# Scaling the exponentials of attention on ScalarE in place of VectorE, in the last group of heads

## The reference

```python
q, k, v = (einsum('bsd,hed->bhse', x, W) for W in (W_Q, W_K, W_V))
scores = einsum('bhse,bhme->bhsm', q, k) / sqrt(128)
scores = where(causal, -1e9, scores)
pattern = softmax(scores, axis=-1)
z = einsum('bhsm,bhme->bhse', pattern, v)
x = layernorm(x + einsum('bhse,hde->bsd', z, W_O))
```

## Time and profile before

| | before |
|---|---|
| median of 3 runs | 1580.17 us (1578.04 to 1580.86) |
| the profiled execution | 1575.68 us, span 1573.5 us |
| TensorE matmul busy | 1489.1 us (95%) |
| VectorE busy | 1122.9 us (71%) |
| ScalarE busy | 744.3 us (47%) |
| GpSimd busy | 504.1 us (32%) |
| chain that ended last | TensorE 47%, issue 22%, VectorE 13%, GpSimd 12%, ScalarE 5% |

### The profile page before, as it was taken

The page is one execution under the profiler, slowest core; times in us unless marked ns, Lnnn a source line. Parts: engine busy times, 40 slices in busy tenths (PEclk is TensorE's granted clock), DMA queues, the critical chain, the costliest instruction groups (busy, mean ns, idle before and its releaser), DMA issues.

```text
span 1573.5 us, 29159 instructions
## 1 busy us (share of the span) xinstructions
PE 1489.1 (95%) x9433; PEld 1303.9 (83%) x9433; DVE 1122.9 (71%) x3031; ACT 744.3 (47%) x1967; POOL 504.1 (32%) x355
## 2 busy tenths in 40 slices
PE   6999999999999988999999999999899799999997
PEld 5989888888989877887888888878688688988886
DVE  5878787887878777655657777867977736442697
ACT  5666666666656544343532263325232544454221
POOL 3323222222322101432347324633673413000650
PEclk9999999999999999999999999999999899999999
DMA  7564646463656203666676457646574788798884
GB/s 274 201 218 169 247 168 228 153 230 136 243 174 222 87 1 130 196 188 178 213 223 203 158 175 218 214 144 193 174 213 167 221 279 286 243 301 265 288 262 143
DMA packets 129737, 315.87 MB, mean 201 GB/s; under 512 B 15968, under 2 KB 39216, under 8 KB 128608
## 3 DMA queue, kind: packets, MB, share of 16 engines
q1 hardware_dynamic: 125024, 301.95, 58.5%
q0 software_dynamic: 4608, 12.59, 2.4%
HBM read 225.35 MB, written 88.60 MB: 200 GB/s over the span
## 4 chain that ended last, share of the span: by engine, by line
PE 47%; issue 22%; DVE 13%; POOL 12%; ACT 5%; DMA 1%; SPq 1%; DVEq 0%; ACTq 0%; POOLq 0%
PE psum L511 40%; POOL act_sb L836 6%; POOL mix L854 3%; POOL xs L866 2%; PE psum L1741 2%; DVE s_sb L1322 1%; PE psum L1752 1%; ACT p_sb L968 1%; PE psum L1731 1%; PE psum L1980 1%; ACT kT_hi L927 1%; DVE s_sb L1320 1%; POOL square_sum L858 1%; DVE kT_lo L1201 1%; DVE pT_lo L1337 1%
## 5 line engine op out<-in xcount | busy, mean ns | idle before, releaser
L511 PE MATMUL psum<-xT_hi,gu_w 128*128 128x512 f32 x1088 | 373.1, 402 | 12.4 <-DVE act_sb L1372 11.6
L836 POOL TENSOR_TENSOR act_sb<-act_sb,comb 128x512 f32<-128x512 f32 x96 | 158.1, 1646 | 375.3 <-DVE act_sb L1372 300.2
L511 PEld LDWEIGHTS psum<-xT_hi,gu_w 128*128 128x128 f32 x1088 | 205.4, 189 | 65.3 <-DVE act_sb L1372 13.2
L1009 ACT ACTIVATE gated<-psum 128x512 f32<-128x512 f32 (+1 forms) x138 | 82.4, 597 | 369.3 <-PE psum L511 367.0
L1372 DVE TENSOR_TENSOR act_sb<-psum,gated 128x512 f32<-128x512 f32 (+1 forms) x138 | 94.9, 688 | 169.9 <-PE psum L511 162.3
L790 POOL TENSOR_TENSOR split_stage<-raw_stage,split_stage 128x768 fp32r<-128x768 f32 x56 | 103.0, 1839 | 351.2 <-ACT split_stage L917 351.2
L511 PE MATMUL psum<-xT_lo,gu_w 128*128 128x512 f32 x544 | 215.5, 396 | 0.0
L511 PEld LDWEIGHTS psum<-d_w,act_hi 128*128 128x128 f32 (+1 forms) x1104 | 149.8, 188 | 13.2 <-issue 1.5
L511 PE MATMUL psum<-d_w,act_hi 128*128 128x256 f32 (+1 forms) x1104 | 154.2, 282 | 0.0
L966 ACT ACTIVATE p_sb<-s_sb,neg_max 128x128 f32<-128x128 f32 x128 | 51.5, 403 | 171.5 <-DVE neg_max L1322 171.3
L511 PEld LDWEIGHTS psum<-xT_lo,gu_w 128*128 128x128 f32 x544 | 102.7, 189 | 18.7
(11 more groups left out here) (257 smaller groups left out, 4021.6 us busy)
## 6 DMA issues: line engine op xcount, KB each, us to landing
gu_w<-w_split SPq DMA_DIRECT2D x138, 512.0 KB, 3.9
w_split<-split_stage SPq DMA_DIRECT2D x56, 768.0 KB, 4.0
d_w<-w_split SPq DMA_DIRECT2D x138, 256.0 KB, 4.0
bw<-l_w SPq DMA_DIRECT2D x63, 496.0 KB, 3.7
xs<-zeros SPq DMA_DIRECT2D x21, 1280.0 KB, 7.5
raw_stage<-w_all SPq DMA_DIRECT2D x56, 384.0 KB, 4.5
decay_all<-decay_dram SPq DMA_DIRECT2D x32, 384.0 KB, 5.5
in_w<-w_split SPq DMA_DIRECT2D x40, 256.0 KB, 4.2
```

The source lines that it names most:

```text
L511: last = nc.tensor.matmul(out_ap, w, m, start=start and n == 0, stop=stop and n == len(pairs) - 1, **kw)
L836: pool.tensor_tensor(act_sb[:, s % 2, :], act_sb[:, s % 2, :], comb[:, comb_block(s) % 2, :], ALU.mult).then_inc(comb_done, 1)
L1009: act.activation(gated[to, s % 2, :], psum[0:to.stop - to.start, G_BANK, :], ACT.Silu).then_inc(gated_ready, 1)
```

## The change

In the last group alone (norm is True there), VectorE keeps the reciprocal but no longer scales. ScalarE scales instead, with two ACTIVATE instructions of the function Identity whose scale is the column row_inv. They stand behind the exponentials of unit i and scale unit i-1; before them ScalarE waits for the reciprocal of unit i-1 (r_ready). The second signals p_scaled, as VectorE's second did.

```diff
--- before.py
+++ after.py
@@ -967,6 +967,11 @@
                                        accum_out=row_sum[:, u % 3, 0:1])
                         act.activation(p_sb[:, u % 3, P:3 * P], s_sb[:, u % 2, P:3 * P], ACT.Exp, bias=neg_max[:, u % 3, 1:2], scale=-1.0,
                                        accum_out=row_sum[:, u % 3, 1:2]).then_inc(p_ready, 1)
+                    if norm and 0 <= i - 1 < UNITS:
+                        u = i - 1
+                        act.wait_ge(r_ready, g * UNITS + u + 1)
+                        act.activation(p_sb[:, u % 3, 0:P], p_sb[:, u % 3, 0:P], ACT.Identity, scale=row_inv[:, u % 3, 0:1])
+                        act.activation(p_sb[:, u % 3, P:3 * P], p_sb[:, u % 3, P:3 * P], ACT.Identity, scale=row_inv[:, u % 3, 1:2]).then_inc(p_scaled, 1)
                     for bp, j in jobs:
                         qkv_high(g, bp, j)
                     if u_t is not None:
@@ -1326,9 +1331,10 @@
                         dve.wait_ge(p_ready, g * UNITS + u + 1)
                         dve.reciprocal(row_inv[:, u % 3, :], row_sum[:, u % 3, :]).then_inc(r_ready, 1)
                         dve.wait_ge(r_ready, g * UNITS + u + 1)
-                        dve.tensor_scalar(p_sb[:, u % 3, 0:P], p_sb[:, u % 3, 0:P], row_inv[:, u % 3, 0:1], None, ALU.mult)
-                        dve.tensor_scalar(p_sb[:, u % 3, P:3 * P], p_sb[:, u % 3, P:3 * P], row_inv[:, u % 3, 1:2], None,
-                                          ALU.mult).then_inc(p_scaled, 1)
+                        if not norm:
+                            dve.tensor_scalar(p_sb[:, u % 3, 0:P], p_sb[:, u % 3, 0:P], row_inv[:, u % 3, 0:1], None, ALU.mult)
+                            dve.tensor_scalar(p_sb[:, u % 3, P:3 * P], p_sb[:, u % 3, P:3 * P], row_inv[:, u % 3, 1:2], None,
+                                              ALU.mult).then_inc(p_scaled, 1)
                     for bp, j in jobs:
                         qkv_low(g, bp, j)
                     if u_t is not None:
```

## The result

The change takes 1590.24 us (median of 4 runs, 1589.08 to 1591.45), the kernel before 1579.41 (4 runs, 1578.04 to 1580.86): a ratio of 1.0073, 95% interval 1.0060 to 1.0086, or 10.8 us slower. The forecast was 1590.3 with +10.1 us.

What follows compares the result with a forecast made beforehand. A ring of dependences through ScalarE's queue, no full engine, was taken to bound the last group. Fifteen turns by 0.71 (10.65) - 1.20 hidden + 0.62 at the end = +10.1 us, 1590.3 us from median 1580.17; range 1585.5 to 1594.5.

Steps and rivals of the forecast that it cites:

- What bounds the group: Last group of heads: no engine is full; a ring of dependences, mostly between VectorE and ScalarE, sets the time.
- The ring: Each turn: VectorE's mask, ScalarE's exponentials and projection copy, then VectorE's low parts and next mask; VectorE's scaling is off it.
- What is removed: VectorE's two scaling instructions in iterations 1 to 15 stand before idle time, so taking them out is worth 0.
- rival (c): VectorE's relief comes through: each of 15 turns 0.46 us shorter, 6.9 us faster, 1573.3 us; chance 0.02.
- the sum engine against engine: The skill's rule as prices: ScalarE's 0.71 less VectorE's 0.46, 16 times, 4.0 us, or 1584.2 us.
- The pair: ScalarE's two added scalings, between exponentials and projection copy, cost 0.71 us a turn; bounds 0.42 and 0.89.
- ScalarE's added wait: Waiting for VectorE's reciprocal costs nothing in iterations 1 to 15; only in iteration 16 must ScalarE wait.
- What TensorE hides: Waits for TensorE in iterations 4, 6 and 8 fill up first and take 1.20 us off the delay.
- The end of the group: Iteration 16, without exponentials: ScalarE waits for the last reciprocal, and TensorE's next transposes start 0.62 us late.
- Rival (a): TensorE's clock falls behind the gap before the transposes at 583.86: 1.5 us on top, 1591.8 us; chance 0.27.
- Rival (b): TensorE hides all of iterations 1 to 8, leaving seven turns and the end: 5.6 us, 1585.8 us; chance 0.08.
- Rival (d): No change, because something behind the group absorbs the delay; chance 0.05.

Runs made afterwards that it cites:

- e2_pair_last: The change, with ScalarE's wait and scaling pair moved behind the last copy of the same iteration; 1605.3 us, ratio 1.0014 to the kernel before.
- e6_idle_pair: Kernel before, plus two unused ScalarE Identity instructions of the same widths behind each unit's exponentials in the last group, without a wait; 1610.09 us, ratio 1.0051.
- e5_no_scaling: Kernel before, but in the last group nobody scales the exponentials and VectorE does not wait for its reciprocal; 1600.91 us, ratio 0.9998.
- e1_no_own_wait: The change, but VectorE no longer waits for its own reciprocal in the last group; 1614.24 us, ratio 1.0076 to the kernel before.
- e3_units_0_7: The change for units 0 to 7 alone, VectorE scaling units 8 to 15 as before; 1608.1 us, ratio 1.0038 to the kernel before.

## Why the prediction was right

The forecast, +10.1 us and 1590.3, was met at +10.8 and 1590.24; the range, 1585.5 to 1594.5, held it. That the absolute time agrees within 0.1 us is luck: the forecast stood on a median of 1580.17, 0.76 above the 1579.41 of the four runs, and its sum was 0.7 too low. By its steps:

- **What bounds the group.** The ring through ScalarE's queue. Shown by e2_pair_last (same work, other position, +1.46 in place of +10.74) and e6_idle_pair (idle work, same position, 0.69 a turn).
- **What is removed: 0.** Shown by e5_no_scaling, 0.9998 and 0.08 us. The predicted idle time of VectorE, near 1.8 us, was 2.01: the removed scaling was worth 0.59 and not 0.46 of waiting, since it ends 0.59 behind the reciprocal's end, and the leftover wait adds 0.07. The forecast hung nothing on the 0.46; the price of rival (c) and the 4.0 us of the sum engine against engine did.
- **The pair: 0.71 predicted, 0.69 measured** (0.29 and 0.40). Taking start to start of the exponentials, and neither copy starts nor whole durations, was right to 0.02 us.
- **ScalarE's added wait: nothing predicted** but at the end. Shown by e6_idle_pair, which has no such wait and the same 0.69 a turn.
- **The term that was missing** is VectorE's leftover wait for its own reciprocal. The prediction does not mention it; its reason, that the reciprocal is long done, was given for ScalarE's wait alone. VectorE never idles for the reciprocal, and yet the wait costs 0.06 to 0.07 us a turn, through the extra entry in VectorE's queue. A turn is 0.76, fifteen are 11.4 where 10.65 was written.
- **What TensorE hides: 1.20 predicted; 1.32 measured** (15 by 0.76 less 10.08). The places were right. The delays grow by 0.46, 0.53, 0.50 and 0.21 behind iterations 4, 5, 6 and 8 in place of 0.76; the missing 0.30, 0.23, 0.26 and 0.55 stand against 0.24, 0.24, 0.24 and 0.48. With the turn of 0.70, in e1_no_own_wait, the hidden part is 14 by 0.70 less 8.60, that is 1.20. TensorE's own lateness, put at 1.42 at 542.07 and some 3 us at 566, was 1.49 at its transposes of 543.60 and 3.35 at those of 563.63.
- **The end of the group: 0.62 predicted, 0.66 measured.** The one wait for the reciprocal, in iteration 16, lasts 0.83 us.
- The sum: 11.40 - 1.32 + 0.66 = 10.74 where 10.65 - 1.20 + 0.62 = 10.1 was written. The turn, 0.02 too long for the pair and 0.07 too short for the leftover wait, is 0.75 of the difference, the hidden part takes 0.12 back, and the end adds 0.04.
- **Rival (a)**, with 0.27, came in its event and not in its price. The gap grew to 3.23 and the granted clock fell to 0.57 for 4 us, but the 1.5 us were not paid, for the turns there cost what the others do while TensorE is idle for 1.86 of 6 us: the argument "slower matmuls first eat its gaps" fits. That the change caused the fall is not shown: the clock fell at this place too in e3_units_0_7 and e5_no_scaling, where the gap is 2.46 and 2.48 us as before (0.66 in 590 to 595 and in 585 to 590 us). The Trainium skill, "TensorE: Matmul & The Clock Gate", section "Why this matters for your kernels", has such gaps lower the clock; the traces of the change agree with that, and show no cost of it.
- **Rival (b)** fell with e3_units_0_7. **Rival (c)**, a gain from VectorE's relief, fell with e5_no_scaling. **Rival (d)** fell with the ratio: its interval begins at 1.0060, clear of no change.
- The rule of the Trainium skill, "ScalarE: Activation LUTs", section "Rules for kernel authors", multiplications on VectorE, names the right engine here, but the difference of prices (4.0 us) is not what is paid: 10.8 us are, and with the pair in another queue position 1.46.
- **The range** took in "the 2 us by which runs of the kernel before differ"; the three runs lie 2.8 us apart. Nothing hung on this.

What stays open: whether other engines pay as much when two waits stand ahead of one instruction; no run has that.

## What to carry to other kernels

When no engine is full, look for the ring and ask of every instruction only whether it stands on it: here work off the ring was worth nothing when removed, and the same work on it cost its start-to-start time in each turn that TensorE did not hide. Within a queue, put first what another engine waits for next and the long work behind it; here that order alone, in all eight groups, gave 1.05% with the same instructions. When an instruction is removed, remove its wait too, or it will be carried by the next one.

## What the runs showed of the hardware

- With two waits ahead of it, one of them long met, a VectorE instruction started 0.11 us after the other's releaser ended, with one wait 0.03 us. The second wait shows as an EVENT_SEMAPHORE of 0.02 us in VectorE's queue, and the instruction starts 0.05 us behind it.
- A gap of TensorE of the same 2.48 us had the granted clock at 1.00 behind it in the kernel before and at 0.66 in e5_no_scaling (one trace each, on different chips), by the row of the timeline and that of the stretch:

```profile
584.90 0.52 PE L1743 MATMUL psum<-ident,p_sb 128*128 128x128 f32 x3 [2.48 <-DVE pT_lo L1339]
```

```profile
585.00:590.00 5.00, 4.52 (x28) 4.23 (x28) 3.59 (x16) 1.69 (x7) 0.00 (x0) 0.66 0.00 0
```

It cost nothing there either: the last transposes are 0.08 us late. So in these traces the length of a gap of 2.48 us alone does not tell whether the clock falls behind it.
